# A delta-rule stage in which TensorE computes each group of the next pair's Gram products one slot later

## What is computed

```python
def fw_step(W, inp):
    qt, kt, vt, bt = inp
    v_old = einsum('bhij,bhj->bhi', W, kt)
    W = W + (bt * (vt - v_old))[..., :, None] * kt[..., None, :]
    z = einsum('bhij,bhj->bhi', W, qt)
    return (W, z)
_, z = scan(fw_step, W0, (q, k, v, beta))
```

## Time and profile before

| what | value |
|---|---|
| median of 3 executions | 18497.64 us (18490.13 to 18520.3) |
| the profiled execution's own time | 18509.24 us |
| its span, from first to last instruction | 18507.2 us |
| granted TensorE clock, mean over the span | 0.787 |
| delta stage, first to last projection and solve | about 5660 to 10165 us, a quarter of the span |
| PE busy in the span / DVE / ACT / POOL | 71% / 57% / 35% / 12% |

### The profile page before, as it was taken

The page is one execution under the profiler, slowest core; times in us unless marked ns, Lnnn a source line. Parts: engine busy times, 40 slices in busy tenths (PEclk is TensorE's granted clock), DMA queues, the critical chain, the costliest instruction groups (busy, mean ns, idle before and its releaser), DMA issues. The chain is left out here.

```text
span 18507.2 us, 593329 instructions
## 1 busy us (share of the span) xinstructions
PE 13100.1 (71%) x262069; PEld 10249.8 (55%) x262069; DVE 10585.8 (57%) x24424; ACT 6518.6 (35%) x16019; POOL 2265.2 (12%) x1394
## 2 busy tenths in 40 slices
PE   4607778862847888888888667766677675867777
PEld 3505666651535676766766455555555564735555
DVE  6451457763144555555555676767776745346664
ACT  3101246640214565665665112121211121345541
POOL 0048100003541111111111000000000000000001
PEclk9556578875868999999999667866787697967775
DMA  0313320121331111111111222021211153177752
GB/s 22 106 30 46 69 48 21 33 77 45 65 76 46 24 26 26 26 24 26 26 24 26 47 42 43 19 44 38 45 33 28 38 129 93 39 228 195 195 136 68
DMA packets 1835030, 1095.27 MB, mean 59 GB/s; under 512 B 1109166, under 2 KB 1763409, under 8 KB 1814481
## 3 DMA queue, kind: packets, MB, share of 16 engines
q1 hardware_dynamic: 1605063, 999.32, 22.4%
q0 software_dynamic: 227328, 57.19, 2.1%
HBM read 569.43 MB, written 484.53 MB: 57 GB/s over the span
## 5 line engine op out<-in xcount | busy, mean ns | idle before, releaser
L2894 PE MATMUL recur_acc<-recur_U,recur_W 8*32 8x64 f32 (+4 forms) x49152 | 1402.4, 270 | 510.3 <-ACT recur_W L2816 428.5
L2894 PEld LDWEIGHTS recur_acc<-recur_U,recur_W 8*32 8x32 f32 (+4 forms) x49152 | 1068.8, 140 | 928.8 <-ACT recur_W L2816 738.6
L2945 DVE TENSOR_TENSOR recur_pr<-recur_K,recur_e 124x64 f32<-124x64 f32 (+60 forms) x1024 | 1282.0, 1252 | 395.9 <-ACT recur_e L2828 395.6
L2881 PE MATMUL recur_acc<-recur_R,recur_E 128*32 128x64 f32 x62976 | 1206.6, 232 | 247.1 <-issue 235.4
L2950 DVE TENSOR_REDUCE recur_dot<-recur_pr 124x1 f32<-124x64 f32 (+60 forms) x1024 | 1281.8, 1252 | 29.8
L2881 PEld LDWEIGHTS recur_acc<-recur_R,recur_E 128*32 128x32 f32 x62976 | 1070.1, 118 | 350.0 <-issue 294.0
L2475 ACT ACTIVATE delta_B0l<-delta_pS 64x256 f32<-64x256 f32 x1968 | 743.4, 378 | 875.4 <-PE delta_pS L2375 857.9
L2816 ACT ACTIVATE recur_W<-recur_wT 128x256 f32<-128x256 f32 (+16 forms) x1024 | 335.1, 327 | 1961.2 <-PE recur_wT L2866 1960.0
L2866 PE MATMUL recur_wT<-const_ident,recur_w 128*128 128x128 f32 (+15 forms) x1536 | 479.5, 375 | 768.1 <-DVE recur_w L2954 760.9
L2475 ACT ACTIVATE delta_B1l<-delta_pS 64x256 f32<-64x256 f32 x1968 | 743.6, 378 | 698.8 <-PE delta_pS L2375 678.2
L2375 PE MATMUL delta_pM<-delta_B1l 64*64 64x128 f32 (+1 forms) x11808 | 737.2, 255 | 140.8 <-ACT delta_B1l L2478 140.3
(11 more groups left out here) (620 smaller groups left out, 34022.7 us busy)
## 6 DMA issues: line engine op xcount, KB each, us to landing
scr<-rel_BD SPq DMA_DIRECT2D x128, 1288.0 KB
rel_sc<-scr SPq DMA_DIRECT2D x128, 861.0 KB
xnT<-ln_xT SPq DMA_DIRECT2D x64, 492.0 KB, 3.0
kr<-delta_QK SPq DMA_DIRECT2D x492, 64.0 KB, 2.4
ur<-delta_Uf SPq DMA_DIRECT2D x492, 64.0 KB, 2.3
zz<-delta_Z SPq DMA_DIRECT2D x492, 64.0 KB, 2.2
recur_K<-kr SPq DMA_DIRECT2D x64, 448.0 KB
recur_H<-zz SPq DMA_DIRECT2D x64, 448.0 KB
```

The lines of the kernel that those rows point to most:

```text
L2881: nc.tensor.matmul(acc[a][32 * q:32 * q + 32, 0:FD], E[a][:, EQ * q + 32 * j:EQ * q + 32 * j + 32], R[a][:, m, :], start=(j == 0), stop=False)
L2894: ins = nc.tensor.matmul(acc[a][32 * q:32 * q + 32, 0:FD], W[a][0:8 * k, b, 160 * q + 32 * j:160 * q + 32 * j + 32], U[a][0:8 * k, 2 * (t ...
L2945: V.tensor_tensor(pr[0:cp, 0:n, :], K[a][0:cp, r0:r0 + n, :], e[a][0:cp, None, :].to_broadcast([cp, n, FD]), ALU.mult).then_inc(s_own[a], 1)
```

## The change

```diff
         PROJ_AT = {0: 0, 1: 1, 2: 2, 3: 3, 4: 4}
         TURN_AT = {16: 0, 17: 1, 18: 2}
-        GRAM_AT = {19: 0, 20: 1, 21: 2, 22: 3, 23: 4, 24: 5}
+        GRAM_AT = {20: 0, 21: 1, 22: 2, 23: 3, 24: 4, 25: 5}
         PROJ_READ = {s + 1: j for s, j in PROJ_AT.items()}
         TURN_READ = {s + 1: j for s, j in TURN_AT.items()}
         MASK_AT = {s + 1: j for s, j in GRAM_AT.items() if j < 5}
```

## The result

The changed kernel takes 18442.11 us (median of 8 executions, 18429.46 to 18454.94), the kernel before 18501.24 in the same number (18490.13 to 18520.3). The ratio is 0.9966 with a 95% interval of 0.9955 to 0.9977: 0.34% faster, 59 us, where 0.47% was forecast. Timed again beside the kernel before on a chip on which that one takes 18577 us, the ratio is 0.9958 (0.9944 to 0.9971).

A forecast was written before the change was run, and what follows sets the result against it. It took PE's hand-written order, its work plus waits, to bound the delta stage. Gaining 0.71 us a pair over 122 pairs gave 87 us: 18497.64 - 87 = 18411 us, range 18370 to 18468.

The forecast's parts named there:

- The mechanism: Slots 19 to 26: the head of slot 20 runs inside Gram 0's wait for KT, gaining 0.71 us a pair.
- The bubble: PE's idle 1.17 us before Gram 0, filled by slot 20's head; Gram 0 still starts at 17.97.
- a Gram group occupies PE for 0.38 before the next job starts; a tail ... 0.38 too: On PE, slots 19 to 26: each group or tail of 16 matmuls takes 0.38 us before the next job.
- The estimate by the Trainium skill's figure for a matmul that stands alone: On PE's exposed waits: 0.19 us charged once more, leaving a gain of 0.52 a pair, 63 us.
- The waits: On PE: DVE's masks L2595 over 100 us, at Gram 3 and 5; Gram 0 still waiting about 0.4 for KT.
- The rest: ACT's, POOL's and SP's programs keep their order, costed at nothing; other stages unchanged.
- The lower bound: Slots 23 and 25: DVE operations without overlap and waits of 0.15 leave a gain of about 0.3 a pair, 37 us.
- Rival A: Slots 23 and 25: DVE chains behind heads give back the bubble's gain; 18461 to 18498 us; chance 0.12 with C.
- Rivals B and C: B: masks crowd DVE in slots 24 to 26, slower, 0.04. C: slot 20's head waits too, 18498 us, 0.01.
- the new waits: On PE: Gram 3 waits 0.50 and Gram 5 0.84 for masks behind heads' readings, 1.34 us together.

The follow-up runs named there:

- e1: The changed kernel with DVE's masks left in their old slots 20 to 24: ratio 0.9905 to the kernel before, pairs 33.73 us apart.
- e2: The kernel before with Gram group 0 alone moved behind the head of slot 20: ratio 0.9922, pairs 34.13 us apart.
- e8: Against the kernel before, Gram groups two slots later, masks 0 to 4 in their groups' slots, next pair's columns copied early: ratio 0.9864, pairs 33.02 us apart.

## Why the prediction was right, and by how much it was off

The mechanism held step by step; one of its terms was mis-sized. In us after the pair's copy to `xc` (7992.78 in the earlier trace rows, 7988.60 after):

```
                               worked out   measured
slot 20, head ends             24.86        24.90
Gram 0 starts                  25.19        25.19
slot 22, head starts           26.33        26.50
Gram 3 starts                  28.70        28.87
slot 24, head starts           29.08        29.17
slot 24, head ends             30.22        30.43
Gram 5 starts                  31.45        31.64
slot 26, head starts           31.83        31.94
pair                           34.64        34.80
```

**The bubble.** "The bubble is filled; its remainder is still there": right. Gram 0 starts to the hundredth where it did, with the head in front of it. The Trainium skill (TensorE: Matmul & The Clock Gate, Step-by-step: what each phase is for) says that weight loads can be pulled ahead and that matmuls stay in program order. On the order of jobs the traces agree: in the earlier trace rows the head of slot 20, whose squares were copied by 8014.03, starts at 8018.35, only behind Gram 0, though PE stood idle from 8016.80, and it starts 1.4 us ahead of Gram 0 when the program has it first. Record by record they don't quite: after the change that head's first records start at 8012.35, before the last two of the tail ahead of it, at 8012.40.

**The step that was off: "a Gram group occupies PE for 0.38 before the next job starts; a tail ... 0.38 too".** Measured by itself a group costs 0.48. The 0.38 is the distance of first records, and a group's records come in two rows of 8, for the two halves of the partitions, each 0.058 us behind the last of its row; where one half is ahead, its next job starts before the other half has ended. Gram 0, a tail and Gram 1 in a row (slots 20 and 21) show the difference: 26.50 - 25.19 = 1.31 us from Gram 0 to the head of slot 22 in place of 3 x 0.38 = 1.14, so that head is 0.17 late. The head of slot 24 was taken at 1.14 and lasts 8019.03 - 8017.77 = 1.26; the rows of before had it at that length too (8023.47 to 8024.73), so a measure taken from one head was used for another. Against this, PE went from Gram 3 and Gram 5 to a head in 0.30 rather than 0.38, twice. Together: 0.17 + 0.12 - 0.16 = 0.13 at the head of slot 26, measured 0.11. The other 0.05 of the 0.16 missing arise between that head and the pair's end, where I had taken the order as unchanged; they were not traced further. The mechanism was right; that it came out this close is in part luck, since the 0.16 that two Gram groups cost less made up for about half of the 0.29 that the others cost more.

The estimate by the Trainium skill's figure for a matmul that stands alone (TensorE: Matmul & The Clock Gate, Single matmul latency), charged once more, was 0.52 a pair, and 0.55 is nearer to that than to 0.71. That is luck as far as the runs show: the terms above account for most of the difference, and PE's resumption after a mask still takes 0.06 (8017.41 to 8017.47, 8020.18 to 8020.24). The page gives the figure for bf16 on the full array, and the row that it was compared with is the median of all Gram records, most of which don't stand alone.

**The waits.** Right in kind and place (Gram 3 and Gram 5, none at Gram 4, KT's remainder; Gram 2 too starts 0.06 behind its masks, 8015.63 + 0.41 = 8016.04 and 8016.10, with no idle time shown), and wrong in how they would show: I expected more than 100 us on L2595 and 0.4 at KT, and the view has 57.7 and 0.29. I had counted from the moment when PE could have started the next job, the view counts from the end of the last record. The chain, not the count of idle time, is what to compare.

**The rest.** The other engines' programs cost nothing that shows: PE's waits for ACT's copies of the squares sum to 216 us before and 217 after (6000 to 10000). The clock did not move, nor did the other stages beyond the spread. The lower bound (0.3, from DVE operations without overlap) was far off the truth: they kept 0.34 and 0.33. Rival A's chains did give back two thirds of the 1.62 that e1 shows to be there, but not all. Rivals B and C have nothing for them: DVE still idles 1.02 us before it reads the head of slot 24, Gram 5 waits 0.28, and the head of slot 20 did move up.

**What the prediction didn't ask** is what each half of the edit is worth. It priced the new waits at 1.34 and then accepted them as part of the change; that `MASK_AT` follows `GRAM_AT` by one slot was a property of how the table is written, and e1 shows that it need not be so: leaving the masks alone gets 1.07 of it back.

## What to carry to other kernels

In an order written by hand, fill a bubble by moving the group that waits (e2), and its followers too where they gain by it (e1), but ask of what consumes their results by itself where it should stand: here the whole table took the masks along, from behind a short job's reading to behind a long one's, and that gave back two thirds of the gain. When a job moves past another, look on the consumer's engine at what stands in front of the operation that frees the buffer, not at how busy that engine is (DVE is busy 59% of a pass here, and its masks set the pair's length all the same). For the price of a group of small matmuls that run in two halves, issue one twice (0.48 here), or take the distance over several in a row (1.31 / 3 = 0.44); the distance of two first starts (0.38) is too small.

## What was not expected

As PE's waits shrink, irregular stalls grow: 34 pairs were longer than the undisturbed distance before and 94 in e8, and what they sum to grew from 21 to 68 us, 47 us of the 284 that its undisturbed distance promises (122 x 2.33). In e8's delta stage PE sat idle for 0.25 to 5 us before 56 of its matmul records with nothing shown that it waited for (6 before the change); 47 of the 56 stand over 28 us after the pair's start, at its end. The DMA view counts the loads of instructions, here over 516 us of e8's delta stage, 7409 to 7925 (queue, kind, packets, MB, share):

```profile
q8 instruction: 101, 1.65, 1.4%
```

That is a load of 16 KB every 5.1 us. Of the 56 records 40 start between 1.20 and 1.45 us after the last such load has landed; before the change it is 4 of 6. If the two had nothing to do with each other, about one in twenty would. This points to PE running out of instructions, the faster its order becomes. But the loads may themselves follow PE's progress, and no run here tests it, so it stays open.
